# Splitting the first adjacency block of a GNN layer with layer norm into two halves, with seven warm-up matmuls instead of ten

## The chip, the cores and the metric

The kernel runs on one core of a Trainium2 chip. The metric is the device time of one execution in microseconds (us), here the median of three runs; the profile comes from one further, profiled execution. TensorE does the matrix products, VectorE (DVE), ScalarE (ACT) and GpSimd (POOL) the elementwise work, SyncE (SP) issues nearly all DMAs.

## The reference

```python
support = x @ weight                                   # x: 4096 x 256, weight: 256 x 256
g = (1.0 - t) * support + t * (adj @ support)          # adj: 4096 x 4096
out = layernorm(x + g)                                 # over the 256 features, eps 1e-5
```

All data are float32. The adjacency is sparse in values but stored dense, 64 MB.

## The kernel before

The kernel uses that the product with the weights can come last: it computes z = t * (x^T adj^T) + (1 - t) * x^T for 512 columns (nodes) at a time, a **chunk**, and then multiplies z by the weights, adds x and normalises. There are eight chunks; each sums over the 4096 nodes in 32 **blocks** of 128, grouped four at a time into eight **groups**. One block of one chunk is a 128 x 512 piece of the transposed adjacency, 256 KB.

Precision is kept with split operands: every float32 operand is rounded to a high part (type fp32r, which TensorE takes at one pass) and a low part (the rest). A product is then three matmuls: high x high, high x low, low x high. The features give two tiles of 128 (`KT = 2`), so a block costs six matmuls of 512 columns, each behind a load of 128 x 128 weights, here a tile of x.

**Who does what.** SP issues the loads in one fixed order. ScalarE makes the high part of the adjacency (L257 for the first pieces, L263 for whole groups). VectorE makes its low part by a subtraction (L464 for the first pieces, L359 for groups), once the high part is there. For the first four blocks of x, VectorE casts the high part (L423) and GpSimd subtracts for the low part (L335); later x pieces are cast by ScalarE (L253) and subtracted by VectorE (L428). TensorE multiplies. Each engine works through its own program in order; semaphores tie them together.

**The start.** Chunks 0 and 1 are computed side by side, since both need the same x. Their first pieces are small, so that work can start early: `A_PIECES` lists (slot, block, count) for 12 adjacency pieces, of which the first eight are single blocks, in turn for chunk 0 and chunk 1; `X_PIECES` lists those of x. All of them lie packed in one array `in_first_run`, in the order in which they are loaded (`FIRST_RUN`: x0, a0, a1, x1, a2, a3, x2, a4, a5, x3, a6, a7, ...), and SP issues one DMA for each, x0 at L204 and a0 at L205. The host lays this array out, and that is not part of the time.

TensorE begins with `WARM = 10` matmuls of constants in bf16, 512 columns each (L675 to L677), into `out_ps[0]`, whose contents nobody reads. Then come the first four pieces, a0 to a3, in `fine_piece` (L565): it waits for the high parts and multiplies high x high (L573), then waits for the low part of x (L577), then for that of the adjacency (L581). From the fifth piece, a4, on, `piece` (L584) waits for all operands at once and multiplies in another order (L561, L562, L563). From group `n = 4` on, `group` (L599) does whole groups from adjT; slots are a ring of four.

**The first block, a0, is special before the change as well.** It arrives in one DMA, but two engines cast it, so that its high part is there sooner:

```python
# ScalarE, L277
act.wait_ge(a0_loaded[0], 16)
nc.scalar.activation(a_hi[:, 0, 0, 0:WIDE // 2], a_raw[:, 0, 0, 0:WIDE // 2], ACT.Copy).then_inc(a0_hi_ready, 1)
# VectorE, L467
x_high(0)
dve.wait_ge(a0_loaded[0], 16)
nc.vector.tensor_copy(a_hi[:, 0, 0, WIDE // 2:], a_raw[:, 0, 0, WIDE // 2:]).then_inc(first_hi_ready, 1)
dve.wait_ge(first_hi_ready, 1)
a_low_piece(0)
```

After a0, VectorE's order is a1 low, x1 high, a2 low, a3 low, x2 high, a4 low, a5 low, x3 high, a6 low, a7 low. GpSimd only does the low parts of x0 to x3 there, each as soon as VectorE has cast it.

SP's first wait within the loads is that of the first whole group (L182): it waits until VectorE has made the low parts of all pieces in the slot that is loaded again.

Of the kernel before, what the change touches and what calls it, by code (L numbers as in the profile page):

```python
# [6 lines left out]
P = 128  # L7
WIDE = 512
GROUP = 4
RING = 4  # L10
X_RING = 3
W_TURN = 6
WARM = 10
FINE = 4
# [9 lines left out]
def gnn_layernorm_kernel(nc, x_rows, first_run, xT, adjT, t, W, out):  # L24
# [33 lines left out]
    with ctx:  # L58
# [3 lines left out]
        def sem(name):  # L62
            return ctx.enter_context(nc.semaphore(name))
# [47 lines left out]

        first_hi_ready = sem("first_hi_ready")
        w_loaded, w_hi_ready, w_lo_ready = sem("w_loaded"), sem("w_hi_ready"), sem("w_lo_ready")
# [33 lines left out]
        def x_part(buf, p):  # L147
            j, n = X_PIECES[p]
            return buf[:, j // GROUP % X_RING, j % GROUP:j % GROUP + n]

        def run_offset(kind, index):
            ahead = FIRST_RUN[:FIRST_RUN.index((kind, index))]
            return sum(P * X_PIECES[i][1] * feats if which == "x" else P * A_PIECES[i][2] * WIDE for which, i in ahead)
# [6 lines left out]
        def adj_source(q):  # L160
            n = A_PIECES[q][2]
            first = run_offset("a", q)
            return first_run[first:first + n * P * WIDE].rearrange("(p b w) -> p b w", p=P, b=n)

        def load_and_store(sp):
# [12 lines left out]
            def load_adj(n):  # L178
                slot, turn = n % RING, n // RING
                c, g = chunk_group(n)  # L180
                if turn == 1:
                    sp.wait_ge(a0_lo_ready, a_after(slot))  # L182
                else:
                    sp.wait_ge(a_lo_ready[slot], turn - 1)
# [19 lines left out]
            load_x(0)  # L204
            load_adj_piece(0)  # L205
            load_adj_piece(1)
# [42 lines left out]
        def scalar_engine(act):  # L249
# [22 lines left out]
            def root(c):  # L272
# [3 lines left out]
            act.preload_act_table_set("sqrt_and_others")  # L276
            act.wait_ge(a0_loaded[0], 16)  # L277
            nc.scalar.activation(a_hi[:, 0, 0, 0:WIDE // 2], a_raw[:, 0, 0, 0:WIDE // 2], ACT.Copy
                                 ).then_inc(a0_hi_ready, 1)
            for q in range(1, A_EARLY):  # L280
# [74 lines left out]
        def vector_engine(dve):  # L355
# [100 lines left out]
            def centre_rows(c):  # L456
                for i in range(TILES):
                    dve.wait_ge(x_mean_ready, i + 1)
                    nc.vector.tensor_scalar(rows[:, c % 2, i], rows[:, c % 2, i], mean_var[:, i, 0:1], None, ALU.subtract
                                            ).then_inc(x_centred, 1)  # L460

            def a_low_piece(q):
                dve.wait_ge(a0_hi_ready, q + 1)
                nc.vector.tensor_tensor(a_part(a_lo, q), a_part(a_raw, q), a_part(a_hi, q).bitcast(f32), ALU.subtract  # L464
                                        ).then_inc(a0_lo_ready, 1)

            x_high(0)  # L467
            dve.wait_ge(a0_loaded[0], 16)
            nc.vector.tensor_copy(a_hi[:, 0, 0, WIDE // 2:], a_raw[:, 0, 0, WIDE // 2:]).then_inc(first_hi_ready, 1)
            dve.wait_ge(first_hi_ready, 1)  # L470
            a_low_piece(0)
            for p in range(1, EARLY):
# [84 lines left out]
        def tensor_engine(pe):  # L557
            def products(c, slot, j, b, k, first, last):
# [4 lines left out]
                return nc.tensor.matmul(bank, x_lo[:, j, cols], a_hi[:, slot, b], start=False, stop=last)  # L563

            def fine_piece(q):  # L565
                slot, b, _ = A_PIECES[q]
                bank = agg[slot % 2]
                pe.wait_ge(x0_hi_ready, b + 1)
                pe.wait_ge(a0_hi_ready, q + 1)
                if q == 0:  # L570
                    pe.wait_ge(first_hi_ready, 1)
                for k in range(KT):
# [3 lines left out]
                for k in range(KT):  # L576
                    nc.tensor.matmul(bank[k][:, :], x_lo[:, b, k * P:(k + 1) * P], a_hi[:, slot, b],  # L577
                                     start=False, stop=False)
                pe.wait_ge(a0_lo_ready, q + 1)
                for k in range(KT):  # L580
# [3 lines left out]
            def piece(q):  # L584
                slot, first, count = A_PIECES[q]
                c, g = chunk_group(slot)
                pe.wait_ge(a0_lo_ready, q + 1)
                if g == 0:
# [86 lines left out]
            for _ in range(WARM):  # L675
                nc.tensor.matmul(out_ps[0][:, :], nc.const_aps.tensor(1.0, [P, P], bf16),  # L676
                                 nc.const_aps.tensor(1.0, [P, WIDE], bf16), start=True, stop=True)  # L677
            for q in range(FINE):
                fine_piece(q)
# [48 lines left out]
```

## Time and profile before

| | us |
|---|---|
| median of 3 runs | 383.89 (383.85 to 384.13) |
| the profiled execution | 383.85 |
| its span, first to last instruction | 382.6 |
| TensorE busy | 376.6, 98% of the span |
| VectorE busy | 237.6, 62% |
| ScalarE busy | 145.7, 38% |
| GpSimd busy | 22.2, 6% |
| read from HBM over the span | 79.95 MB, 220 GB/s |

Times within the trace are microseconds from the start of the span. PE is the matmul side of TensorE and PEld its weight loads, which overlap matmuls; SPq is SyncE's queue, where the time of a DMA row is that of its issue, not of the transfer. Matmuls are pipelined: the recorded start of one can lie ahead of its streaming, and its end is modelled. A row "x10" merges ten instructions of a kind. What stands in brackets at a row's end is the idle time of that engine before it and what ended it.

### The profile page before, as it was taken

The numbers are of one execution on the slowest core, as the hardware profiler recorded it, in microseconds if no ns is written. First come the engines' busy times: TensorE is split into PE (matmuls) and PEld (weight loads), VectorE is DVE, ScalarE is ACT, GpSimd is POOL, SyncE is SP. The second block draws the span as 40 slices with busy tenths as digits, with TensorE's granted clock in tenths as the row PEclk, the third lists the DMA queues.
The fourth block names the chain that finished last, engine by engine and source line by source line (L and its number), as shares of the span: only waits on it lengthen the run. The fifth ranks groups of instructions, "written<-read, shape, count | busy, mean of one in ns | idle before, by whom it ended". The sixth has DMA issues, their size and how long they took to land.

```text
span 382.6 us, 4167 instructions
## 1 busy us (share of the span) xinstructions
PE 376.6 (98%) x1686; PEld 310.8 (81%) x1686; DVE 237.6 (62%) x335; ACT 145.7 (38%) x114; POOL 22.2 (6%) x19
## 2 busy tenths in 40 slices
PE   9999999999999999999999999999999999999994
PEld 5888888888888888888888888888888888888884
DVE  4978955447879466844577446873477643697305
ACT  4767544243352434324424325244332344423102
POOL 1202300003000010000100001000100001000000
PEclk9999999999999999999999999999999999999999
DMA  7999997555465766557665666756647567321001
GB/s 258 418 392 418 415 420 265 190 217 207 179 231 208 257 217 233 184 214 258 218 202 194 208 244 212 243 197 213 212 179 274 174 267 270 119 106 55 2 0 56
DMA packets 19107, 84.42 MB, mean 221 GB/s; under 512 B 1936, under 2 KB 6800, under 8 KB 11408
## 3 DMA queue, kind: packets, MB, share of 16 engines
q1 hardware_dynamic: 18656, 83.89, 59.7%
q10 hardware_dynamic: 432, 0.26, 0.2%
q8 instruction: 13, 0.21, 0.2%
q14 instruction: 6, 0.05, 0.0%
HBM read 79.95 MB, written 4.19 MB: 220 GB/s over the span
## 4 chain that ended last, share of the span: by engine, by line
PE 98%; DVE 1%; ACT 0%; issue 0%; DVEq 0%
PE agg L563 30%; PE agg L562 30%; PE agg L561 30%; PE out_ps L624 3%; PE out_ps L625 2%; PE out_ps L676 1%; PE agg L573 1%; PE agg L577 1%; PE agg L581 0%; ACT x_raw L325 0%; DVE x_raw L529 0%; DVE stats L533 0%; PE out_ps L645 0%; PE out_ps L647 0%; PE out_ps L646 0%
## 5 line engine op out<-in xcount | busy, mean ns | idle before, releaser
L359 DVE TENSOR_TENSOR a_lo<-a_raw,a_hi 128x2048 fp32r<-128x2048 f32 x60 | 137.4, 2291 | 111.1 <-ACT a_hi L263 111.1
L561 PE MATMUL agg<-a_hi,x_hi 128*128 128x512 f32 x504 | 196.3, 389 | 0.0
L563 PE MATMUL agg<-a_hi,x_lo 128*128 128x512 f32 x504 | 196.2, 389 | 0.0
L562 PE MATMUL agg<-a_lo,x_hi 128*128 128x512 f32 x504 | 196.1, 389 | 0.0
L263 ACT ACTIVATE a_hi<-a_raw 128x2048 fp32r<-128x2048 f32 x60 | 114.7, 1913 | 129.0 <-PE agg L563 123.7
L561 PEld LDWEIGHTS agg<-a_hi,x_hi 128*128 128x128 f32 x504 | 94.6, 188 | 19.8
L563 PEld LDWEIGHTS agg<-a_hi,x_lo 128*128 128x128 f32 x504 | 94.6, 188 | 19.8
L562 PEld LDWEIGHTS agg<-a_lo,x_hi 128*128 128x128 f32 x504 | 94.6, 188 | 19.6
L340 POOL TENSOR_TENSOR xt<-xt,omt_col 128x1024 f32<-128x1024 f32 x8 | 18.1, 2257 | 292.4 <-DMA xt<-in_xT 292.4
L624 PE MATMUL out_ps<-w_split,z_hi 128*128 128x512 f32 x56 | 20.0, 397 | 0.0
L274 ACT ACTIVATE std<-var_eps 128x4 f32<-128x4 f32 x7 | 1.4, 206 | 47.7 <-DVE var_eps L400 47.7
L270 ACT ACTIVATE z_hi<-z 128x512 fp32r<-128x512 f32 x14 | 8.8, 633 | 26.8 <-DVE z L372 21.7
L625 PE MATMUL out_ps<-w_split,z_lo 128*128 128x256 f32 x56 | 15.7, 280 | 0.0
L464 DVE TENSOR_TENSOR a_lo<-a_raw,a_hi 128x512 fp32r<-128x512 f32 (+1 forms) x12 | 11.3, 961 | 2.6 <-ACT a_hi L257 2.2
L624 PEld LDWEIGHTS out_ps<-w_split,z_hi 128*128 128x128 f32 x56 | 10.5, 188 | 2.5
L372 DVE SCALAR_TENSOR_TENSOR z<-agg,t_col,xt 128x512 f32<-128x512 f32 x14 | 10.4, 747 | 2.8 <-PE agg L563 2.8
L378 DVE TENSOR_TENSOR z_lo<-z,z_hi 128x512 fp32r<-128x512 f32 x14 | 9.5, 688 | 2.7 <-ACT z_hi L270 2.1
L625 PEld LDWEIGHTS out_ps<-w_split,z_lo 128*128 128x128 f32 x56 | 10.6, 189 | 0.3
L428 DVE TENSOR_TENSOR x_lo<-x_raw,x_hi 128x1024 fp32r<-128x1024 f32 (+1 forms) x8 | 10.5, 1310 | 0.1
L257 ACT ACTIVATE a_hi<-a_raw 128x512 fp32r<-128x512 f32 (+1 forms) x11 | 8.7, 789 | 4.7 <-DMA a_raw<-in_first_run 4.6
L387 DVE TENSOR_TENSOR x_raw<-out_ps,rows 128x256 f32<-128x256 f32 x28 | 9.9, 416 | 0.0
L391 DVE TENSOR_TENSOR x_raw<-out_ps,x_raw 128x256 f32<-128x256 f32 x28 | 9.9, 415 | 0.0
(76 smaller groups left out, 95.9 us busy)
## 6 DMA issues: line engine op xcount, KB each, us to landing
a_raw<-in_adjT SPq DMA_DIRECT2D x60, 1024.0 KB, 4.8
xt<-in_xT SPq DMA_DIRECT2D x8, 512.0 KB, 5.6
rows<-in_x SPq DMA_DIRECT2D x8, 512.0 KB, 5.7
out<-x_raw SPq DMA_DIRECT2D x7, 512.0 KB, 2.9
x_raw<-in_first_run SPq DMA_DIRECT2D x6, 512.0 KB, 11.9
a_raw<-in_first_run SPq DMA_DIRECT2D x8, 256.0 KB, 4.6
a_raw<-in_first_run SPq DMA_DIRECT2D x4, 512.0 KB, 7.3
x_raw<-in_first_run SPq DMA_DIRECT2D x4, 128.0 KB, 3.9
```

The lines of the kernel that those rows point to most:

```text
L263: nc.scalar.activation(a_hi[:, slot], a_raw[:, slot], ACT.Copy).then_inc(a_hi_ready[slot], 1)
L340: nc.gpsimd.tensor_tensor(xt[:, c % 2], xt[:, c % 2], omt_col[:, :].unsqueeze(2).broadcast_to([P, KT, WIDE]), ALU.mult).then_inc(xt_scaled, 1)
L359: nc.vector.tensor_tensor(a_lo[:, slot], a_raw[:, slot], a_hi[:, slot].bitcast(f32), ALU.subtract).then_inc(a_lo_ready[slot], 1)
L372: nc.vector.scalar_tensor_tensor(z[:, k], agg[c % 2][k][:, :], t_col[:, :], xt[:, c % 2, k], ALU.mult, ALU.add).then_inc(z_ready[k], 1)
L387: nc.vector.tensor_tensor(y_tile(i), out_ps[i][:, 0:feats], rows[:, c % 2, i], ALU.add).then_inc(part_ready, 1)
L428: nc.vector.tensor_tensor(x_lo[:, j:j + n], x_part(x_raw, p), x_hi[:, j:j + n].bitcast(f32), ALU.subtract).then_inc(x_lo_ready, 1)
L464: nc.vector.tensor_tensor(a_part(a_lo, q), a_part(a_raw, q), a_part(a_hi, q).bitcast(f32), ALU.subtract).then_inc(a0_lo_ready, 1)
L561: nc.tensor.matmul(bank, x_hi[:, j, cols], a_hi[:, slot, b], start=first, stop=False)
L562: nc.tensor.matmul(bank, x_hi[:, j, cols], a_lo[:, slot, b], start=False, stop=False)
L563: return nc.tensor.matmul(bank, x_lo[:, j, cols], a_hi[:, slot, b], start=False, stop=last)
L624: nc.tensor.matmul(out_ps[i][:, :], z_hi[:, k, cols], w_split[:, k], start=(k == 0), stop=False)
L625: done = nc.tensor.matmul(dst, z_lo[:, k, cols], w_hi[:, k], start=False, stop=(k == KT - 1))
```

## The change

a0 is loaded by two DMAs, columns 0 to 255 and 256 to 511, each with a semaphore of its own; the host lays the two halves out one behind the other. VectorE casts the first half and ScalarE the second, each when its half is there. VectorE subtracts for the low part in two instructions of 256 columns instead of one of 512. TensorE multiplies a0 in a new function, `first_piece_half`: for each half two matmuls high x high, two low x high and two high x low, twelve matmuls of 256 columns with twelve weight loads instead of six and six. `WARM` is 7 instead of 10. The count `a0_lo_ready` now gets two increments from a0, so all later waits on it ask for one more, and `a0_hi_ready` gets none from a0, so waits on it ask for one less.

```diff
 W_TURN = 6
-WARM = 10
+WARM = 7
+HALF = WIDE // 2
 FINE = 4
...
 
-        first_hi_ready = sem("first_hi_ready")
+        half_loaded, half_hi_ready = sems("half_loaded", 2), sems("half_hi_ready", 2)
         w_loaded, w_hi_ready, w_lo_ready = sem("w_loaded"), sem("w_hi_ready"), sem("w_lo_ready")
...
 
+        def first_block(buf, h):
+            return buf[:, 0, 0, h * HALF:(h + 1) * HALF]
+
         def run_offset(kind, index):
...
             return first_run[first:first + n * P * WIDE].rearrange("(p b w) -> p b w", p=P, b=n)
+
+        def first_block_source(h):
+            first = run_offset("a", 0) + h * P * HALF
+            return first_run[first:first + P * HALF].rearrange("(p w) -> p w", p=P)
...
                 if turn == 1:
-                    sp.wait_ge(a0_lo_ready, a_after(slot))
+                    sp.wait_ge(a0_lo_ready, a_after(slot) + 1)
                 else:
...
             load_x(0)
-            load_adj_piece(0)
+            for h in range(2):
+                sp.dma_start(first_block(a_raw, h), first_block_source(h)).then_inc(half_loaded[h], 16)
             load_adj_piece(1)
...
             act.preload_act_table_set("sqrt_and_others")
-            act.wait_ge(a0_loaded[0], 16)
-            nc.scalar.activation(a_hi[:, 0, 0, 0:WIDE // 2], a_raw[:, 0, 0, 0:WIDE // 2], ACT.Copy
-                                 ).then_inc(a0_hi_ready, 1)
+            act.wait_ge(half_loaded[1], 16)
+            nc.scalar.activation(first_block(a_hi, 1), first_block(a_raw, 1), ACT.Copy).then_inc(half_hi_ready[1], 1)
             for q in range(1, A_EARLY):
...
 
+            def a_low_half(h):
+                dve.wait_ge(half_hi_ready[h], 1)
+                nc.vector.tensor_tensor(first_block(a_lo, h), first_block(a_raw, h), first_block(a_hi, h).bitcast(f32),
+                                        ALU.subtract).then_inc(a0_lo_ready, 1)
+
             def a_low_piece(q):
-                dve.wait_ge(a0_hi_ready, q + 1)
+                dve.wait_ge(a0_hi_ready, q)
                 nc.vector.tensor_tensor(a_part(a_lo, q), a_part(a_raw, q), a_part(a_hi, q).bitcast(f32), ALU.subtract
                                         ).then_inc(a0_lo_ready, 1)
 
             x_high(0)
-            dve.wait_ge(a0_loaded[0], 16)
-            nc.vector.tensor_copy(a_hi[:, 0, 0, WIDE // 2:], a_raw[:, 0, 0, WIDE // 2:]).then_inc(first_hi_ready, 1)
-            dve.wait_ge(first_hi_ready, 1)
-            a_low_piece(0)
+            dve.wait_ge(half_loaded[0], 16)
+            nc.vector.tensor_copy(first_block(a_hi, 0), first_block(a_raw, 0)).then_inc(half_hi_ready[0], 1)
+            for h in range(2):
+                a_low_half(h)
             for p in range(1, EARLY):
...
 
+            def first_piece_half(h):
+                cols = slice(h * HALF, (h + 1) * HALF)
+                pe.wait_ge(x0_hi_ready, 1)
+                pe.wait_ge(half_hi_ready[h], 1)
+                for k in range(KT):
+                    nc.tensor.matmul(agg[0][k][:, cols], x_hi[:, 0, k * P:(k + 1) * P], first_block(a_hi, h),
+                                     start=(h == 0), stop=False)
+                pe.wait_ge(x0_lo_ready, 1)
+                for k in range(KT):
+                    nc.tensor.matmul(agg[0][k][:, cols], x_lo[:, 0, k * P:(k + 1) * P], first_block(a_hi, h),
+                                     start=False, stop=False)
+                pe.wait_ge(a0_lo_ready, h + 1)
+                for k in range(KT):
+                    nc.tensor.matmul(agg[0][k][:, cols], x_hi[:, 0, k * P:(k + 1) * P], first_block(a_lo, h),
+                                     start=False, stop=False)
+
             def fine_piece(q):
                 slot, b, _ = A_PIECES[q]
                 bank = agg[slot % 2]
                 pe.wait_ge(x0_hi_ready, b + 1)
-                pe.wait_ge(a0_hi_ready, q + 1)
-                if q == 0:
-                    pe.wait_ge(first_hi_ready, 1)
+                pe.wait_ge(a0_hi_ready, q)
                 for k in range(KT):
...
                                      start=False, stop=False)
-                pe.wait_ge(a0_lo_ready, q + 1)
+                pe.wait_ge(a0_lo_ready, q + 2)
                 for k in range(KT):
...
                 c, g = chunk_group(slot)
-                pe.wait_ge(a0_lo_ready, q + 1)
+                pe.wait_ge(a0_lo_ready, q + 2)
                 if g == 0:
...
                                  nc.const_aps.tensor(1.0, [P, WIDE], bf16), start=True, stop=True)
-            for q in range(FINE):
+            for h in range(2):
+                first_piece_half(h)
+            for q in range(1, FINE):
                 fine_piece(q)
...
             slot, b, n = A_PIECES[index]
-            first_run.append(adjT[slot % 2 * (blocks // GROUP) + slot // 2, :, b:b + n].ravel())
+            halves = [slice(0, HALF), slice(HALF, WIDE)] if index == 0 else [slice(0, WIDE)]
+            for cols in halves:
+                first_run.append(adjT[slot % 2 * (blocks // GROUP) + slot // 2, :, b:b + n, cols].ravel())
     first_run = np.concatenate(first_run)
     arrays = {"in_x": x_rows, "in_first_run": first_run, "in_xT": xT, "in_adjT": adjT, "in_t": L0_gnn_t, "in_W": L0_gnn_weight}
     arrays = {name: np.ascontiguousarray(a) for name, a in arrays.items()}
```

## Rows read from the trace of the kernel before

**Rows 1.** The page: the chain that ended last, share of the span by engine.
```profile
PE 98%; DVE 1%; ACT 0%; issue 0%; DVEq 0%
```

**Rows 2.** The chain in order of time, 0 to 12 us: start, duration, engine, tile, line.
```profile
0.84 4.42 PE out_ps L676 x10
5.26 0.85 PE agg L573 x2
6.12 0.65 PE agg L577 x2
...
7.68 0.45 PE agg L577 x2
```

**Rows 3.** Timeline, 0.8 to 4.3: start, duration, engine, line, operation. SP issues, last warm-up load.
```profile
0.81 0.38 SPq L173 DMA_DIRECT2D x_raw<-in_first_run  x1
...
1.25 0.89 SPq L176 DMA_DIRECT2D a_raw<-in_first_run  x2
...
2.65 0.91 SPq L176 DMA_DIRECT2D a_raw<-in_first_run  x2
...
4.21 0.15 PEld L676 LDWEIGHTS out_ps<-const-bfloat16-1.0 128*128 128x128 bf16 x1 [0.28 <-issue]
```

**Rows 4.** Timeline, 4.6 to 5.4: TensorE's first real loads.
```profile
4.63 0.76 PEld L573 LDWEIGHTS agg<-a_hi,x_hi 128*128 128x128 f32 x2 [0.28 <-issue]
...
5.06 0.33 PEld L573 LDWEIGHTS agg<-a_hi,x_hi 128*128 128x128 f32 x1
```

**Rows 5.** Timeline, 2.9 to 5: casts and subtractions of x0 and of a0.
```profile
2.95 0.29 DVE L423 CAST x_hi<-x_raw 128x256 fp32r<-128x256 f32 x1 [2.95 <-DMA x_raw<-in_first_run]
3.33 0.73 POOL L335 TENSOR_TENSOR x_lo<-x_raw,x_hi 128x256 fp32r<-128x256 f32 x1 [2.82 <-DVE x_hi L423]
...
3.80 0.40 DVE L469 CAST a_hi<-a_raw 128x256 fp32r<-128x256 f32 x1 [0.55 <-DMA a_raw<-in_first_run]
...
4.32 0.69 DVE L464 TENSOR_TENSOR a_lo<-a_raw,a_hi 128x512 fp32r<-128x512 f32 x1
...
4.94 0.63 ACT L257 ACTIVATE a_hi<-a_raw 128x512 fp32r<-128x512 f32 x1 [0.73 <-DMA a_raw<-in_first_run]
```

**Rows 6.** Timeline, 9.3 to 12: low parts of fifth and seventh block, fifth block's first load.
```profile
9.38 0.74 POOL L335 TENSOR_TENSOR x_lo<-x_raw,x_hi 128x256 fp32r<-128x256 f32 x1 [2.06 <-DVE x_hi L423]
9.40 1.27 DVE L464 TENSOR_TENSOR a_lo<-a_raw,a_hi 128x512 fp32r<-128x512 f32 x1
...
10.92 0.19 PEld L561 LDWEIGHTS agg<-a_hi,x_hi 128*128 128x128 f32 x1
...
11.40 0.68 DVE L464 TENSOR_TENSOR a_lo<-a_raw,a_hi 128x512 fp32r<-128x512 f32 x1
```

**Rows 7.** Timeline, 374.1 to 375.2: matmuls of 256 columns in the last projection.
```profile
374.10 0.28 PE L646 MATMUL out_ps<-w_split,z_hi 128*128 128x256 f32 x1
...
375.07 0.28 PE L645 MATMUL out_ps<-w_split,z_hi 128*128 128x256 f32 x1
```

**Rows 8.** Timeline, 7 to 8.5: second block's first matmuls, third block's cast and loads.
```profile
7.07 0.62 PE L573 MATMUL agg<-a_hi,x_hi 128*128 128x512 f32 x2
7.10 0.63 ACT L257 ACTIVATE a_hi<-a_raw 128x512 fp32r<-128x512 f32 x1 [1.53 <-DMA a_raw<-in_first_run]
...
8.20 0.41 PEld L573 LDWEIGHTS agg<-a_hi,x_hi 128*128 128x128 f32 x2
```

**Rows 9.** Timeline, 12 to 14: SP's first issue behind the first run.
```profile
12.11 1.48 SPq L185 DMA_DIRECT2D a_raw<-in_adjT  x2
```

**Rows 10.** Stretches of one us: busy time of each engine; last the DMA share, GB/s.
```profile
4.00:5.00 1.00, 1.00 (x4) 0.48 (x2) 0.88 (x2) 0.27 (x2) 0.05 (x1) 1.00 1.05 364
5.00:6.00 1.00, 1.00 (x4) 0.74 (x3) 0.41 (x2) 0.57 (x1) 0.00 (x0) 1.00 0.87 285
```

**Rows 11.** Timeline, 23 to 27.3: first adjT group's low part, and its first load.
```profile
23.38 2.29 DVE L359 TENSOR_TENSOR a_lo<-a_raw,a_hi 128x2048 fp32r<-128x2048 f32 x1 [2.13 <-ACT a_hi L263]
...
27.24 0.19 PEld L561 LDWEIGHTS agg<-a_hi,x_hi 128*128 128x128 f32 x1
```

## The prediction

> **What bounds the kernel now.** I read the engine table and the chain that ended last first: TensorE is busy for 98% of the span, and so is the chain [rows 1]. So only what moves TensorE's stream counts, and it counts in full, because no later stage absorbs it. Then the chain in order of time for the first 12 us [rows 2]: ten warm-up matmuls until 5.26, then block after block of real products, with no pause. The reader is to see the spacing there: two matmuls of 512 columns take 0.85 at 5.26 and 0.45 from 7.68 on. The profile's own column of the granted clock shows 1.00 throughout, but 512 columns in 0.427 are TensorE at 1.2 GHz and in 0.227 at 2.4 GHz; the pair that takes 0.65 holds the step, so the clock rises at about 6.4, some 5.5 us after the first warm-up matmul at 0.84.
>
> The recorded ends lie about 0.2 behind the streaming: a matmul starts when the load behind it is recorded (the last warm-up load, at 4.21, starts with the ninth; the first real one, at 4.63, with the tenth [rows 3, 4]), so the tenth warm-up starts at 4.63 and streams to 5.06, and real columns stream from 5.06 [rows 4]. From there I compare, block by block, when TensorE wants an operand with when it is ready.
>
> **The change, part by part.** *Three warm-ups less.* 3 x 0.427 = 1.28 us of slow streaming goes; the seventh ends at 5.06 - 1.28 = 3.78. The warm-up did double duty: it covered the wait for data and brought the clock up. If the clock still rises at 6.4, each slow microsecond won is worth half, since its columns would otherwise run at 2.4 GHz: the most that can be won is 0.64 us. That alone is below what a measurement of this kernel can tell from no change (about 0.2%, 0.77 us).
>
> *The first half's arrival and cast.* The first x piece is issued at 0.81 and cast from 2.95, 2.14 later; the first adjacency block is issued at 1.25 and cast from 3.80 [rows 3, 5]. Half of it carries as much as that x piece, so it lands at about 3.35: 1.25 + 2.14 = 3.39, or 3.80 less 0.45. VectorE then casts it: 0.29 alone, 0.40 beside GpSimd [rows 5]. GpSimd's x_lo runs from 3.33 to 4.06 [rows 5], so the two meet head on. Ready time: from 3.65 (0.29, unhindered) to 4.20 (it gets through only behind GpSimd, as the old cast did, which ended 0.14 after GpSimd). I take 4.1, since GpSimd is released 0.06 after the x cast and is likelier to be first. With 0.05 for the wait and a cold load of 0.33 [rows 4], first real columns stream at about 4.4 instead of 5.06, with a pause of about 0.6 behind the last warm-up. Gain so far (1.28 - 0.6) / 2 = 0.34; with the early cast the pause is some 0.1 plus a short wait for x_lo, and the gain about 0.5.
>
> The Trainium skill ("SBUF — State Buffer", "Who interferes with whom") says that VectorE and GpSimd share one pair of ports, which is locked for a whole instruction by whichever starts first. By that rule the first-half cast ends at 4.06 + 0.14 = 4.20 if GpSimd was first, and delays GpSimd if it was not; the sum above would be 0.3 or 0.5. The trace agrees: the low-part subtraction that starts 0.02 after GpSimd takes 1.27 instead of 0.69 [rows 6].
>
> *Six matmuls become twelve of 256 columns, with twelve weight loads.* At 2.4 GHz the last projection shows the pitch: from 374.10 to 375.07 are eight of them, 0.121 each [rows 7], against 0.227 for 512, so 0.015 more a pair. At 1.2 GHz none is in the trace: from below 0.213 each (half of 0.427, nothing added), from above 0.333 (bound by the cold load [rows 4]). I take 0.22, as everything at 2.4 GHz doubled gives at most 0.242. About nine fall before 6.4: 0.06 slow, 0.03 of effect, plus 0.02 after: 0.05. At 0.333 each, the block would end at 4.4 + 6 x 0.333 = 6.4, then 6 x 0.121 = 7.13, against 7.07 before, where the next block's first matmul starts [rows 8]: then all the gain is gone, and 0.06 more.
>
> *One more DMA, and every issue of SP behind it 0.45 later.* SP issues one each 0.44 to 0.47 (0.81, 1.25, and two more to 2.14 [rows 3]); 17 further loads of the first run are queued behind them without a wait, so through by some 10, and the next issue waits until 12.11 anyway for a low part [rows 9], so nothing from there on moves. Before that: pieces land later and later after their issue (a block issued at 2.65 is cast from 7.10 [rows 3, 8]), and the DMA share is 1.05 in 4 to 5 and 0.87 in 5 to 6 [rows 10]. So the lag is hidden by the backlog. It costs only what the transfers cost more: 1 KB rows instead of 2 KB, two starts instead of one. From below 0 (some engines idle in 5 to 6), from above 0.45, the lag itself, if the backlog did not cover it. I take 0.05, nearest to the full stretch.
>
> *What is late next.* Moving TensorE forward uses up the slack of the next blocks, whose operands come by DMA and do not move. (a) Third block: its high part is cast from 7.10 to about 7.74 and its first load is at 8.20 [rows 8]: 0.38 of slack with the wait. (b) Fifth block, the first that wants all three operands at once: its low part runs from 9.40 to 10.67 on VectorE, and its first load is at 10.92 [rows 6]; with 0.04 for the wait, 0.21 of slack. After that it widens: the seventh block's low part ends at 12.08 and is wanted two blocks of 1.36 behind 10.92, at 13.64 [rows 6]; the first adjT group's ends at 25.67, wanted at 27.24 [rows 11]. So whatever the front brings, **what arrives behind the fifth block is at most 0.21**, less the 0.05 of the DMAs: about 0.15. The casts and subtractions in halves are themselves covered: ScalarE is free until 4.94, when a1 has come, and VectorE until a1 is cast, 0.63 later [rows 5]; two subtractions, of at least 0.35 each (half of 0.69 [rows 5]), end at about 5.1, needed then or later. If that cover went, each 0.1 would cost 0.05.
>
> **The sum.** The profiled execution took 383.85 (span 382.6 and 1.25 around it). 0.34 - 0.05 of front gain, cut to 0.21 - 0.05 at the fifth block: 383.85 - 0.15 = **383.7**. The median of the runs is 383.89, 0.04 above the profiled one, which changes nothing.
>
> **Rivals.** *A, the forecast (0.60):* 383.6 to 383.85; the front gains 0.3 to 0.5 and the fifth block takes most of it back.
>
> *B, the cap is lifted (0.17).* The fifth block's subtraction starts 0.02 after GpSimd's x_lo and pays 0.58 for it [rows 6]. For: the seventh, under the same pairing, started first and took 0.68 [rows 6]; a small shift of landings can turn the order. Then the third block's slack and the front decide: 0.33 to 0.5, so 383.35 to 383.5. Against: both follow the same x cast, and what is upstream of them barely moves.
>
> *C, the added DMA is not hidden (0.13).* If all blocks land 0.45 later, the fifth block's low part is ready at 11.16 instead of 10.71, TensorE's load moves from 10.92 to 11.16, and the time is 384.1; with a change in how the 16 DMA engines fall behind, 384.3. For: the share of 0.87 in 5 to 6. Against: the full share in the stretch before it [rows 10].
>
> *D, slower: the clock rises later (0.09).* Place: the pause of up to 0.6 at 3.8 to 4.4, followed by half-width matmuls. Before, the rise came after TensorE had worked without a pause from 0.84 to 6.4. If after the pause it came only behind as long a stretch again, it would stand at 9.9 instead of 6.4: 3.5 us more at half speed, 1.75 lost, less 0.64 for the warm-ups, plus 0.3 for the pause: 383.85 + 1.4 = 385.25. It decides as soon as the rise is some 2.2 us later ((0.77 + 0.34) x 2, as a slow microsecond costs half). For: the warm-up is there for the clock. Against: TensorE is busy nine tenths of the stretch from 0.84 to 6.4 all the same. The Trainium skill ("TensorE: Matmul & The Clock Gate", "What's actually happening") says that the throttled state is the default and activity releases it; that speaks for D as far as a pause counts as missing activity. No row of before holds such a pause.
>
> *E, it doesn't do what it says (0.01):* the early half is ready no sooner than 4.2 and the pause swallows all: 383.85 to 383.9.
>
> **The numbers.** The likeliest is A, 383.7. The range 383.2 to 384.3 takes in A, B, C and the bound of the cold half-width matmuls, and leaves out D. Faster by over 0.2% would need more than the 0.64 that is there: 0.03, for a rise of the clock that comes earlier. Slower: D, 0.09. Within 0.2%: 0.88.
>
> **What the profile of after would show.** Warm-up columns end at 3.78 and the first real load stands alone at about 4.1 to 4.2, with idle time ascribed to VectorE or DMA; the first-half cast takes 0.3 to 0.8; the 256-column matmuls sit 0.21 to 0.24 apart before the step, 0.12 after it; the step from slow to fast matmuls is again at 6.4; the second block's first matmul starts at about 6.75 to 6.8 (7.07 before); a wait before the fifth block's first load, which then sits at about 10.75. Wrong would be: slow spacing beyond 7 (D), the third block's cast starting at 7.4 or later (C), the fifth block's subtraction at 0.69 (B), or cold half-width matmuls 0.3 apart.

## The result, and the profile after

| | before | changed |
|---|---|---|
| median | 383.62 (22 executions, 382.88 to 384.13) | 384.17 (22 executions, 383.80 to 385.18) |
| profiled execution | 383.85, span 382.6 | 384.48, span 383.2 |

The ratio of the times is 1.0019, with a 95% interval of 1.0013 to 1.0025: the change makes the kernel slower by 0.55 us of 384 by the medians and 0.7 by the ratio, less than 0.2% but clearly. The three executions behind the 383.89 above are among the 22 of the kernel before. Six of the executions behind this document, one of them of the kernel before, took 474.58 to 1786.83 us; the ratios leave them out, they move no median by more than 0.04, and the profiles of f1 and f3, which are among them, are not used.

The chain that ended last, of the changed kernel, is no longer TensorE alone (page, share of the span by engine; [rows 1] before):

```profile
PE 95%; DMA 1%; DVE 1%; SPq 1%; ACT 0%; issue 0%; DVEq 0%
```

In order of time, 0 to 14 us, it shows where the rest sits (start, duration, what; [rows 2] before):

```profile
4.07 0.43 SPq L181
4.54 5.21 DMA a_raw<-in_first_run
9.78 0.64 ACT a_hi L266
10.45 1.18 DVE a_lo L477
...
11.67 0.49 PE agg L574
```

Until 11.67 the end is set by data: SP's issues, a block that lands 5.2 us after its issue, its cast, its subtraction. Only then does TensorE take over and run to the end without a gap. Before, TensorE's own stream was the chain from 0.84 on. The part from there on costs the same whatever the kernel: in the 14 profiles used here whose fifth block is multiplied in the old order (all but those of f1 to f4), the execution's time less the start of the fifth block's first load is 372.8 to 373.1. So the kernels differ in what lies ahead of that load, and a microsecond lost there is a microsecond of the result. The timeline of the changed kernel, 2.9 to 6.5, shows the front (columns as in [rows 3 to 5]):

```profile
3.12 0.91 SPq L184 DMA_DIRECT2D a_raw<-in_first_run  x2
3.40 0.72 POOL L343 TENSOR_TENSOR x_lo<-x_raw,x_hi 128x256 fp32r<-128x256 f32 x1 [2.89 <-DVE x_hi L431]
3.42 0.85 DVE L482 CAST a_hi<-a_raw 128x256 fp32r<-128x256 f32 x1
...
4.39 0.50 PEld L583 LDWEIGHTS agg<-a_hi,x_hi 128*128 128x128 f32 x2 [1.31 <-issue]
4.42 0.77 PE L583 MATMUL agg<-a_hi,x_hi 128*128 128x256 f32 x2 [0.43 <-DVE a_hi L482]
4.43 0.42 ACT L287 ACTIVATE a_hi<-a_raw 128x256 fp32r<-128x256 f32 x1 [2.34 <-DMA a_raw<-in_first_run]
...
4.77 0.54 PEld L587 LDWEIGHTS agg<-a_hi,x_lo 128*128 128x128 f32 x2
...
5.20 0.45 PEld L591 LDWEIGHTS agg<-a_lo,x_hi 128*128 128x128 f32 x2
...
5.82 0.30 PEld L587 LDWEIGHTS agg<-a_hi,x_lo 128*128 128x128 f32 x2
...
6.05 0.31 PEld L591 LDWEIGHTS agg<-a_lo,x_hi 128*128 128x128 f32 x2
...
6.41 0.63 PE L600 MATMUL agg<-a_hi,x_hi 128*128 128x512 f32 x2
```

The first half has landed by 3.42 and its cast starts, 0.02 behind GpSimd, so it takes 0.85 and ends at 4.27. The second half has landed by 4.43, one microsecond after the first; in other executions the gap is smaller (cast from 3.92 against 3.43 in this kernel's second profile). At 1.2 GHz two matmuls of 256 columns take 0.43 (from 4.77 to 5.20), at 2.4 GHz 0.23 (5.82 to 6.05). The second block starts at 6.41, against 7.07 before. So the front did get ahead, though part of it is the clock, whose step lies earlier here (see below). Then the loads (timeline, 7 to 12; [rows 8, 6] before):

```profile
7.16 0.63 ACT L266 ACTIVATE a_hi<-a_raw 128x512 fp32r<-128x512 f32 x1 [1.34 <-DMA a_raw<-in_first_run]
...
8.68 0.63 ACT L266 ACTIVATE a_hi<-a_raw 128x512 fp32r<-128x512 f32 x1 [0.88 <-DMA a_raw<-in_first_run]
...
9.78 1.27 ACT L266 ACTIVATE a_hi<-a_raw 128x512 fp32r<-128x512 f32 x2 [0.47 <-DMA a_raw<-in_first_run]
...
10.32 0.74 POOL L343 TENSOR_TENSOR x_lo<-x_raw,x_hi 128x256 fp32r<-128x256 f32 x1 [2.75 <-DVE x_hi L431]
10.45 1.77 DVE L477 TENSOR_TENSOR a_lo<-a_raw,a_hi 128x512 fp32r<-128x512 f32 x2 [0.21 <-ACT a_hi L266]
...
11.66 0.19 PEld L574 LDWEIGHTS agg<-a_hi,x_hi 128*128 128x128 f32 x1 [1.02 <-DVE a_lo L477]
```

The third block's cast (7.16) starts nearly as before (7.10), but TensorE, earlier now, waits some 0.14 for it. The fourth and fifth are cast from 8.68 and 9.78. The fifth's cast started at 8.73 before, so it is 1.05 late: 0.47 of it is SP's later issue (4.54 instead of 4.07), and 0.58 is a longer way from the issue to the cast (5.24 instead of 4.66). Then its low part ends at 11.62 instead of 10.67, and its first load is at 11.66 instead of 10.92. TensorE idles 0.58 there, and the end follows: 384.48 against 383.85.

Where the DMAs fall behind shows in single microseconds (last two columns: share of the 16 engines' time, GB/s). From 3 to 4, first the kernel before, then the changed one:

```profile
3.00:4.00 1.00, 1.00 (x4) 0.37 (x3) 0.45 (x2) 0.20 (x1) 0.67 (x1) 1.00 1.02 289
3.00:4.00 1.00, 0.98 (x3) 0.08 (x1) 0.87 (x2) 0.00 (x0) 0.60 (x1) 1.00 0.65 156
```

The 16 engines stand idle for a third of this stretch and move 156 GB/s instead of 289; in the changed kernel's second profile the share there is 0.91, and they still move only 200. The changed kernel from 5 to 8 ([rows 10] before):

```profile
5.00:6.00 1.00, 1.00 (x8) 1.00 (x8) 0.46 (x2) 0.63 (x1) 0.00 (x0) 1.00 1.04 272
6.00:7.00 1.00, 1.00 (x8) 0.91 (x8) 0.75 (x2) 0.00 (x0) 0.17 (x1) 1.00 0.87 214
7.00:8.00 1.00, 1.00 (x6) 0.53 (x4) 0.17 (x1) 0.63 (x1) 0.57 (x1) 1.00 0.99 307
```

From 6 to 7 it moves 214 GB/s at a share of 0.87, where the kernel before moved 285 at the same share from 5 to 6 [rows 10]. So the share does not tell how much is moved, and a share near 1 is no proof of a backlog that hides an issue. Summed from the start, the kernel before has moved 0.93 MB by 5 us and 1.54 by 7, the changed one 0.79 and 1.28.

### The profile page after: what moved, and what is told of

It is laid out like the page before. It is cut to its first block, busy times and chain, and to the rows that moved or that the text cites. A ratio compares the mean times of both kernels' runs of the same rounds, so it can differ in the third digit from the quotient of the medians.

```text
span 383.2 us, 4175 instructions
## 1 busy us (share of the span) xinstructions
PE 376.3 (98%) x1689; PEld 310.3 (81%) x1689; DVE 238.8 (62%) x336; ACT 145.9 (38%) x114; POOL 22.0 (6%) x19
## 4 chain that ended last, share of the span: by engine, by line
PE 95%; DMA 1%; DVE 1%; SPq 1%; ACT 0%; issue 0%; DVEq 0%
PE agg L574 30%; PE agg L576 30%; PE agg L575 30%; PE out_ps L651 3%; PE out_ps L652 2%; DMA a_raw<-in_first_run 1%; SPq L184 0%; SPq L181 0%; DVE a_lo L477 0%; SPq L214 0%; ACT x_raw L333 0%; DVE x_raw L542 0%; DVE stats L546 0%; ACT a_hi L266 0%; PE out_ps L672 0%
## 5 line engine op out<-in xcount | busy, mean ns | idle before, releaser
L651 PEld LDWEIGHTS out_ps<-w_split,z_hi 128*128 128x128 f32 x56 | 10.5, 188 | 2.5
L436 DVE TENSOR_TENSOR x_lo<-x_raw,x_hi 128x1024 fp32r<-128x1024 f32 (+1 forms) x8 | 10.5, 1308 | 0.0
L425 DVE TENSOR_SCALAR x_raw<-x_raw,mean_var,rstd 128x256 f32<-128x256 f32 x28 | 9.7, 409 | 0.3
```

The lines of the kernel that those rows point to most:

```text
L436: nc.vector.tensor_tensor(x_lo[:, j:j + n], x_part(x_raw, p), x_hi[:, j:j + n].bitcast(f32), ALU.subtract).then_inc(x_lo_ready, 1)
L651: nc.tensor.matmul(out_ps[i][:, :], z_hi[:, k, cols], w_split[:, k], start=(k == 0), stop=False)
```

## The experiments

All times are medians in us; the kernel before was timed beside each group of experiments (383.61 with e1 to e4, 383.53 with e5 to e8, 383.55 with e10 and e11, 383.48 with f1 to f4). "Fifth" is the start of the fifth block's cast, then the end of its low part, then its first load on TensorE, from each kernel's own profile.

| | median | ratio to before, 95% | fifth: cast / low part / load |
|---|---|---|---|
| before, changed | 383.62, 384.17 | 1.0019 (1.0013 to 1.0025) | 8.73 / 10.67 / 10.92, and 9.78 / 11.62 / 11.66 |
| e1_warm7 | 383.46 | 0.9998 (0.9986 to 1.0009) | 8.06 / 9.41 / 10.80 |
| e2_split_warm10 | 384.23 | 1.0014 (1.0005 to 1.0024) | 9.86 / 11.76 / 11.81 |
| e3_one_dma_1kb | 383.46 | 1.0003 (0.9990 to 1.0015) | 8.26 / 10.17 / 10.22 |
| e4_two_dmas | 383.97 | 1.0008 (1.0000 to 1.0017) | 8.96 / 10.89 / 11.13 |
| e5_partition_halves | 384.48 | 1.0022 (1.0014 to 1.0031) | 10.61 / 11.96 / 12.02 |
| e6_tiny_dma | 383.94 | 1.0012 (1.0003 to 1.0021) | 9.72 / 11.08 / 11.13 |
| e7_half_on_scalar | 384.99 | 1.0038 (1.0024 to 1.0053) | 8.88 / 10.2 / 10.95 |
| e8_x_on_scalar_split | 384.38 | 1.0016 (1.0003 to 1.0029) | 9.29 / 10.9 / 11.57 |
| e10_one_dma_a0_a1 | 384.07 | 1.0025 (1.0012 to 1.0038) | 8.70 / 10.1 / 11.42 |
| e11_one_dma_a0_a1_warm9 | 384.23 | 1.0037 (1.0022 to 1.0052) | 8.48 / 10.0 / 11.10 |
| f1_before_fine6 | 383.55 | 1.0000 (0.9991 to 1.0008) | not used |
| f2_after_fine6 | 383.60 | 1.0003 (0.9994 to 1.0013) | 9.22 / 10.58 / 10.37 |
| f3_warm7_fine6 | 383.56 | 1.0006 (0.9997 to 1.0015) | not used |
| f4_one_dma_1kb_fine6 | 383.41 | 1.0006 (0.9993 to 1.0019) | 8.79 / 10.15 / 10.5 |

**e1: the shorter warm-up alone**, in the kernel before.

```diff
-WARM = 10
+WARM = 7
```

> The kernel before with seven warm-up matmuls, nothing else. Theory (the loss comes from the load stream, which one more DMA pushes back by 0.9 us): landings as before, the fifth block's low part ends at about 10.7, TensorE's first real columns at about 4.3, and the time is 0 to 0.25 us below the kernel before. Rival (the loss comes from TensorE's pause behind the warm-up, at the low clock): 0.2 to 0.6 us slower than before with the fifth block's first load later than 10.92.

No difference: 0.9998. TensorE waits 0.4 for the first cast and nowhere else. The rival that this pause carries the whole loss falls: the interval's upper end, 1.0009, is half of it.

**e2: the changed kernel with the old warm-up.**

```diff
-WARM = 7
+WARM = 10
```

> The changed kernel with ten warm-up matmuls instead of seven. Load-stream theory: the loads are late all the same, the fifth block's first load waits until about 11.6 and the time is that of the changed kernel, 0.4 to 0.7 us above before. Rival (TensorE's pause): the pause is gone, so the time is that of the kernel before within 0.15 us.

As slow as the changed kernel. Its timeline, 9.8 to 12:

```profile
9.86 1.24 ACT L266 ACTIVATE a_hi<-a_raw 128x512 fp32r<-128x512 f32 x2 [0.41 <-DMA a_raw<-in_first_run]
...
11.81 0.19 PEld L574 LDWEIGHTS agg<-a_hi,x_hi 128*128 128x128 f32 x1 [1.02 <-DVE a_lo L477]
```

The same lateness and the same wait, without a pause behind the warm-up: the loss does not come from the seven warm-ups.

**e3: the changed kernel, both halves in one DMA.**

```diff
-            for h in range(2):
-                sp.dma_start(first_block(a_raw, h), first_block_source(h)).then_inc(half_loaded[h], 16)
+            first = run_offset("a", 0)
+            sp.dma_start(a_raw[:, 0, 0, :].rearrange("p (h w) -> p h w", h=2),
+                         first_run[first:first + P * WIDE].rearrange("(h p w) -> p h w", h=2, p=P)
+                         ).then_inc(half_loaded[0], 16)
```

> The changed kernel, but both halves come in one DMA of 256 rows of 1 KB; both casts wait for it. If the number of DMAs does it: landings as before (third block's cast from about 7.1, fifth block's low part ended by 10.8), time at or up to 0.2 us below before. If the narrow rows do it: landings late as in the changed kernel (fifth block's low part at 11.2 to 11.6), time 0.3 to 0.7 us above before.

One DMA with the same 256 rows of 1 KB, the same twelve matmuls, the same casts: the median (383.46) is back at that of the kernel before, and the fifth block is cast from 8.26. The times alone do not prove it: three of the twelve lie at 384.63 to 385.16, and the interval, up to 1.0015, just leaves room for the loss of 0.55.

```profile
8.26 1.35 ACT L268 ACTIVATE a_hi<-a_raw 128x512 fp32r<-128x512 f32 x2 [0.39 <-DMA a_raw<-in_first_run]
...
10.22 0.19 PEld L576 LDWEIGHTS agg<-a_hi,x_hi 128*128 128x128 f32 x1 [0.29 <-DVE a_lo L479]
```

So neither the narrow rows nor TensorE's halves make the blocks late; what is left is the second DMA, which e4 to e6 add by itself.

**e4 and e5: the second DMA alone, in the kernel before.** e4 loads the first block by two DMAs of 256 columns, e5 by two of 64 partitions with rows of 2 KB; in both the old casts wait for both (`a0_loaded[0]` at 32). Their lines, e4's first:

```diff
-            load_adj_piece(0)
+            for h in range(2):
+                first = run_offset("a", 0) + h * P * (WIDE // 2)
+                sp.dma_start(a_raw[:, 0, 0, h * (WIDE // 2):(h + 1) * (WIDE // 2)],
+                             first_run[first:first + P * (WIDE // 2)].rearrange("(p w) -> p w", p=P)
+                             ).then_inc(a0_loaded[0], 16)
```

```diff
-            load_adj_piece(0)
+            for h in range(2):
+                first = run_offset("a", 0) + h * (P // 2) * WIDE
+                sp.dma_start(a_raw[h * (P // 2):(h + 1) * (P // 2), 0, 0, :],
+                             first_run[first:first + (P // 2) * WIDE].rearrange("(p w) -> p w", p=P // 2)
+                             ).then_inc(a0_loaded[0], 16)
```

> The kernel before with ten warm-ups and its old casts and matmuls; only the first block's load is two DMAs of 256 columns, and its casts wait for both. Load-stream theory: the first cast starts at about 4.4, the fifth block's low part ends at 11.2 to 11.7 instead of 10.67, the time is 0.3 to 0.8 us above before. Rival (the halves on TensorE, or its pause): as before within 0.15 us.

> The kernel before, but the first block comes in two DMAs of 64 partitions each with rows of 2 KB, so one more DMA without one row more. If it is the number of DMAs: the third to fifth blocks land 0.2 to 1 us later, the fifth block's low part ends at 10.9 to 11.7, the time is 0.2 to 0.7 us above before. If it needed the narrow rows: as before within 0.15 us.

Both are slower, e4 at the edge of its interval, e5 by more than the changed kernel and more than expected. e4's own profile shows no wait for the fifth block, whose first load follows 0.45 behind the pair of loads before it:

```profile
10.68 0.41 PEld L585 LDWEIGHTS agg<-a_lo,x_hi 128*128 128x128 f32 x2
11.13 0.19 PEld L565 LDWEIGHTS agg<-a_hi,x_hi 128*128 128x128 f32 x1
```

So there the low part missed its forecast (ended at 10.89, not 11.2 to 11.7), and where e4's median loses is not seen in its profile. e5's timeline, 8 to 12.1:

```profile
8.16 1.26 ACT L261 ACTIVATE a_hi<-a_raw 128x512 fp32r<-128x512 f32 x2 [2.26 <-DMA a_raw<-in_first_run]
...
10.61 1.26 ACT L261 ACTIVATE a_hi<-a_raw 128x512 fp32r<-128x512 f32 x2 [1.19 <-DMA a_raw<-in_first_run]
...
12.02 0.19 PEld L565 LDWEIGHTS agg<-a_hi,x_hi 128*128 128x128 f32 x1 [0.50 <-DVE a_lo L468]
```

One more DMA without one row more is enough. But e5 is not e4 with wider rows only: its issues take longer on SP, so that the fifth block's comes 0.92 later than before (4.99 against 4.07), where the changed kernel and e4 have 0.47.

**e6: one more DMA that carries 4 bytes**, behind the first block.

```diff
             load_adj_piece(0)
+            sp.dma_start(spare[0:1, :], t).then_inc(spare_loaded, 16)
```

> The kernel before with one more DMA of 4 bytes behind the first block (into a tile that nobody reads). It has the lag on SP (0.47 us) and next to no transfer. If the lag alone does it: every issue 0.47 later, the fifth block's low part at 11.0 to 11.2, time 0.2 to 0.5 us above before. If it is what a DMA of 128 rows costs at its start on the 16 engines: as before within 0.15 us.

Slower by 0.4, though SP's next issue comes only 0.35 later (2.06 instead of 1.71) and the fifth block's only 0.27 (4.34 instead of 4.07). So the added transfer is not what costs. The fifth block is cast from 9.72, which is 0.99 later than in the first profile of the kernel before, but 0.26 later than in its second (below). Whether SP's lag alone does it, or also the start of a further DMA on the engines, this run does not separate, since a small DMA has both. As in e4, the profile shows next to no wait for the fifth block (load at 11.13, some 0.06 behind its turn); that the median loses there is not shown.

**e7 and e8: the issue taken off SP.** e7 has ScalarE issue the second half, e8 the x pieces 0 to 3, two ahead of the table load and two behind it, in place of SP.

```diff
+            act.dma_start(first_block(a_raw, 1), first_block_source(1)).then_inc(half_loaded[1], 16)
             act.preload_act_table_set("sqrt_and_others")
```

```diff
+            for p in range(2):
+                act.dma_start(x_part(x_raw, p), x_source(p)).then_inc(x_loaded[p], 16)
             act.preload_act_table_set("sqrt_and_others")
+            for p in range(2, 4):
+                act.dma_start(x_part(x_raw, p), x_source(p)).then_inc(x_loaded[p], 16)
```

> The changed kernel, its second half issued by ScalarE at 0.8 us in parallel with SP. The number and size of the DMAs are those of the changed kernel, SP's issues are those of before. If SP's lag does it: landings as before, fifth block's low part at about 10.7, time 0 to 0.4 us below before. If the start of one more DMA costs the same on any queue: third to fifth blocks late as in the changed kernel, time 0.3 to 0.7 us above before.

> The changed kernel with the first four x pieces issued by ScalarE, two ahead of its table load and two behind it, so that SP issues four DMAs less in the first 6 us. A version that might beat both: if issue and start of the DMAs bound the first 10 us, the third to fifth blocks land 0.5 to 1.5 us earlier than in the changed kernel, no block waits for data, and the time is 0.2 to 0.7 us below before. If the 16 DMA engines bound them, landings and time are those of the changed kernel within 0.2 us.

Both miss. In e7 the fifth block is cast from 8.88, near to before, as the lag theory has it, yet the kernel is the slowest of all. Its profile shows one cost: x0 and the first half, which TensorE wants first, come later (cast from 3.40 and 3.87 instead of 3.03 and 3.42), and TensorE idles 0.9. But that execution took 384.05, and what the others spend up to 385.75 on is not seen. In e8 it idles 1.1 for the second block:

```profile
7.30 0.70 PE L600 MATMUL agg<-a_hi,x_hi 128*128 128x512 f32 x2 [1.11 <-ACT a_hi L262]
```

With two queues the order of the landings is no longer the order of the program's need.

**e10 and e11: one DMA less.** a0 and a1 come in one DMA of 512 KB with ten and, in e11, with nine warm-ups (`WARM = 9`).

```diff
-            load_adj_piece(0)
-            load_adj_piece(1)
+            first = run_offset("a", 0)
+            sp.dma_start(a_raw[:, 0:2, 0], first_run[first:first + 2 * P * WIDE].rearrange("(p s w) -> p s w", p=P, s=2)
+                         ).then_inc(a0_loaded[0], 16)
```

> The kernel before, but the first two blocks (a0, a1) come in one DMA of 512 KB: one DMA less, as the changed kernel has one more. If each early DMA costs the stream 0.4 to 0.9 us: third to fifth blocks land 0.3 to 0.9 earlier (fifth block's low part ended by 9.8 to 10.4), a0 is cast at about 4.4 (covered by the ten warm-ups), and the time is 0.1 to 0.4 us below before, since TensorE then runs without a wait. If the loss of the changed kernel had another cause: landings and time as before within 0.1 us.

> The same with nine warm-ups: the version that might beat both. If the earlier landings leave slack at the fifth block, one slow warm-up less (0.43 us) is worth 0.1 to 0.2 us more than the kernel with ten: 0.2 to 0.5 us below before. If the fifth block's data still decide: the time of the kernel with ten.

Both miss. No later block waits, but the pair is cast from 5.57 (expected 4.4), 4.3 after its issue, and TensorE idles 0.8; in e11, with nine warm-ups, it is cast from 5.25 and TensorE idles 1.4. The fifth block is cast from 8.70 and 8.48, no earlier than in kernels with one DMA for each. So "each early DMA costs the same" is too simple; what is shown is the cost of one added.

**e12 and e13: both kernels once more**, for a second profile.

> The kernel before once more, for a second profile. Expected: a fifth block's low part that ends within 0.4 us of 10.67 and a first load of the fifth block between 10.3 and 11.2; the step from slow to fast matmuls may lie elsewhere than at 6.4, as the profiles so far show it between 3.8 and 6.7.

> The changed kernel once more, for a second profile. If the lateness of its blocks is systematic: low part of the fifth block ended between 11.2 and 11.9 and TensorE waiting for it. If it was chance of one execution: within 0.3 us of 10.67.

They took 384.31 and 384.05. The second profile of the kernel before shows the very wait of the changed one:

```profile
9.46 1.28 ACT L257 ACTIVATE a_hi<-a_raw 128x512 fp32r<-128x512 f32 x2 [0.36 <-DMA a_raw<-in_first_run]
...
11.45 0.19 PEld L561 LDWEIGHTS agg<-a_hi,x_hi 128*128 128x128 f32 x1 [1.02 <-DVE a_lo L464]
```

and that of the changed kernel two, a longer one for the third block's high part, cast from 7.59 here, and a milder one for the fifth's low part:

```profile
8.36 0.70 PE L600 MATMUL agg<-a_hi,x_hi 128*128 128x512 f32 x2 [0.77 <-ACT a_hi L266]
...
11.22 0.19 PEld L574 LDWEIGHTS agg<-a_hi,x_hi 128*128 128x128 f32 x1 [0.32 <-DVE a_lo L477]
```

The 0.77 did not set the time: the fifth block's low part came later still. Landings scatter by several tenths between executions of one kernel, so a single pair of profiles proves little. All of them together do: with one DMA for the first block (before twice, e1, e3, f4) the fifth block is cast from 8.06 to 9.46, mean 8.66; with one DMA more on SP (changed twice, e2, e4, e5, e6, f2) from 8.96 to 10.61, mean 9.63. The added DMA delays it by some 0.97, between means of ranges that overlap. The bytes moved from the start separate the same twelve profiles without overlap: by 5 us 0.91 to 0.93 MB with one DMA and 0.78 to 0.83 with one more, by 7 us 1.48 to 1.62 (mean 1.54) and 1.21 to 1.36 (mean 1.30).

**f1 to f4: the wait taken away**, in the kernel before (f1), the changed one (f2), e1 (f3) and e3 (f4).

```diff
-FINE = 4
+FINE = 6
```

The fifth and sixth block are multiplied in the order of the first four, high parts first, so the low part is wanted 0.9 later.

> The kernel before with FINE = 6: the fifth and sixth block are multiplied in the order of the first four, so their low parts are wanted 0.9 us later. If TensorE of the kernel before waits at the fifth block in many executions (as in its second profile): 0.1 to 0.4 us below before. If it hardly ever waits there: as before within 0.1 us.

> The changed kernel with FINE = 6. If the wait for the fifth block's low part carries the loss: 0.5 to 0.9 us below the changed kernel, so 0 to 0.4 us below before. If later blocks or the pause at the start hold it: within 0.2 us of the changed kernel, 0.4 to 0.6 us above before.

> The kernel before with seven warm-ups and FINE = 6. If the shorter warm-up is worth something once the data do not decide: 0.1 to 0.4 us below before with ten warm-ups and FINE = 6. If the pause and a later clock eat it: the same within 0.1 us or slower.

> The changed kernel with the first block in one DMA of 1 KB rows and FINE = 6. Against the changed kernel with FINE = 6 it has one DMA less and a first half that comes 0.4 us later. If the added DMA still costs where no low part is waited for: 0.1 to 0.4 us below that kernel. If it only ever mattered for that one wait: the same within 0.1 us.

f2 takes back the loss (383.60, ratio 1.0003 to before, where the changed kernel has 1.0019), though its fifth block is late still. What TensorE waits for is now the low part of x, for some 0.4:

```profile
9.22 1.29 ACT L266 ACTIVATE a_hi<-a_raw 128x512 fp32r<-128x512 f32 x2 [0.34 <-DMA a_raw<-in_first_run]
...
11.24 0.30 PEld L604 LDWEIGHTS agg<-a_hi,x_lo 128*128 128x128 f32 x2 [0.45 <-POOL x_lo L343]
```

So the wait for the fifth block's low part carries the changed kernel's loss: the same edit gains nothing in the kernel before (f1, 1.0000). f1, f3 and f4 are all the kernel before within their intervals: the wait costs that one little on average, the shorter warm-up brings nothing even without it, one DMA less (f4 against f2) brings nothing clear once the wait is gone, and no version tried beats the kernel before.

## Why the prediction was wrong

It forecast 0.15 us less and measured is 0.55 more; the 384.17 lies in its range, and "within 0.2%" held, but the sign was wrong.

- *The step that failed: "One more DMA, and every issue of SP behind it 0.45 later ... I take 0.05", with a bound of 0.45 from above.* It measured about 1 at the fifth block (1.05 between the two profiles, 0.97 between the means), twice the bound. The lag itself is 0.47 there, as taken; nothing hid it, and the loads fell behind by about as much again. I took a DMA share near 1, in two stretches of the kernel before, for a backlog that hides the lag. In the changed kernel the engines idle from 3 to 4 (share 0.65), and later the same share of 0.87 moves 214 GB/s where it moved 285; e6 shows that a DMA of 4 bytes costs 0.4 us of time. This is rival C, which I gave 0.13 and priced at +0.25, or +0.45 with a change in how the engines fall behind. Its sign, a third block cast at 7.4 or later, was put too early: in the first profile that cast starts at 7.16, and the lateness shows from the fourth block on.
- *Where it would show was right.* "The fifth block, the first that wants all three operands at once" is where TensorE waits in the changed kernel, e2, e3, e5 and, in its second profile, before; it is not where e4 and e6 wait in theirs. With 0.95 instead of 0.05 in the sum, the load moves from 10.92 to 10.67 + 0.95 + 0.04 = 11.66, the row read above: +0.74 for that pair of executions. Over many it is 0.55 by the medians and 0.7 by the ratio; the kernel before waits there at times too, as in its second profile. That was the second miss: I read 0.21 of slack off one execution as if it were fixed; in the other it is below zero. And SP's first issue behind the first run, which was to stay at 12.11, came at 13.04, with no cost that shows: from the fifth block's load on both kernels take the same time.
- *The front.* By the prediction's reckoning the pause runs from 3.78 to the second cold load, at 4.56 (the pair ends at 4.89 and one takes 0.33 [rows 4]), as real columns began at the second load (5.06) before: 0.78 (predicted 0.6; the records of the matmuls, with their modelled ends, show 3.99 to 4.42, 0.43), cast ended at 4.27 (4.1 taken, 4.20 as bound). The prediction's own terms give 4.1 + 0.05 + 0.33 = 4.48, not 4.4, so a pause of 0.7 and a gain of 0.29 instead of 0.34; the cap of 0.21 stood below either. The cast started 0.02 behind GpSimd and ended 0.15 behind GpSimd's end at 4.12, as the old one had ended 0.14 behind. By the Trainium skill ("SBUF — State Buffer", "Who interferes with whom") whichever of VectorE and GpSimd starts first holds their shared ports for its whole instruction; the trace agrees, with a cast of 0.85 instead of 0.29. Cold matmuls of 256 columns are 0.21 apart (0.22 taken; the bound of 0.333 is out). The second block starts 0.66 earlier, but 0.44 of it is the clock step at 5.5 instead of 6.4, chance of the execution. Against the second profile of before, whose step is near 5.1, it is 6.41 against 6.46, which leaves some 0.25 for the front with the clock set equal, near the 0.29 (0.34 - 0.05) of the sum. None of it is seen at the end: e1, f2 and f3 are no faster than the kernel before.
- *The clock.* I took the step at 6.4 as a property of the kernel. It moves from execution to execution, in the kernel before from 6.4 to near 5.1; the second profile of the changed kernel has fast pairs from the first on:

```profile
4.40 0.48 PE L583 MATMUL agg<-a_hi,x_hi 128*128 128x256 f32 x2 [0.58 <-DVE a_hi L482]
4.71 0.40 PE L587 MATMUL agg<-a_hi,x_lo 128*128 128x256 f32 x2
4.95 0.40 PE L591 MATMUL agg<-a_lo,x_hi 128*128 128x256 f32 x2
```

- *Rival D, a later rise of the clock,* is in no profile. The times hint at it where the pause is long: of e11's twelve executions (TensorE idle for 1.4 in its profile) five lie at 385.6 to 386.2 and the others at 383.9 to 384.4; of e10's twelve (idle for 0.8) two lie at 386.1 and 386.3 and the others at 384.0 to 384.3. The kernel before has none above 384.41 in 139 executions. That is argued, not shown, since every profile happened to fall among the shorter times; it stays open whether it adds to the changed kernel's upper end of 385.18 or to e7.
- *Rival B,* the subtraction that starts ahead of GpSimd, happened in e1, e7, e8, e10, e11, f2 and f4 (e1: low part done 1.35 after the start of the cast instead of 1.94); in e5 and e6 the two did not overlap at all. None of them is clearly faster than the kernel before.

Left open: by what a small added DMA delays the ones behind it, SP's lag or its start on the engines; where the medians of e4 and e6 lose, since their profiles show no wait; and why e7's times lie 0.9 above its own profiled 384.05.

## What to carry to other kernels

Splitting an early load so that compute can start sooner also adds a DMA to a queue whose later entries may have less slack than the first; look for the first consumer that wants all its operands at once, and price the added DMA there, not at zero because the DMA share is near 1. The bytes moved up to a given time told the two kinds of kernel apart where the share and single landings did not. Slack of a few tenths read off one execution is not slack: landings and the clock step scatter by as much, so take two profiles before building on it. Where a consumer can take its operands in the order in which they get ready (here FINE = 6), that took the wait away where an earlier start did not, but it gained only where this was what the kernel waited for.

## What was unexpected

- One DMA of 4 bytes early on SP costs 0.4 us at the end (383.94 against 383.53, ratio 1.0012).
- From the fifth block's first load on, 14 profiles of 12 kernels take the same time within 0.3 us (372.8 to 373.1).
- The second half, issued 0.47 after the first, is cast 1.0 later in one execution (4.43 against 3.42) and 0.5 later in the other (3.92 against 3.43).
- Moving a 128 KB load to ScalarE's queue at 0.8 us made the changed kernel another 0.8 slower (384.99 against 384.17), without one byte more; that is 1.46 above the kernel before beside it (383.53).
- A pair of blocks in one DMA of 512 KB was there 4.3 us after its issue; the first of them alone takes 2.5 [rows 3, 5].
- TensorE's step from 1.2 to 2.4 GHz lies before 4.7 in one execution of the same code and at 5.5 in another.
